# A Mamba mixer: the z products moved into ACT's silu pass, and the D skip moved to its own chunk

## The chip, the cores and the metric

One core of a Trainium2 chip runs the whole kernel in one launch. The metric is the device time in microseconds, lower is better; a number given as "the time" is the median over runs. The engines are PE (TensorE, matrix products), DVE (VectorE), ACT (ScalarE), POOL (GpSimd) and SP (which issues DMAs).

## The reference, cut to what matters

The kernel computes one block of a network on x of shape (8, 1024, 256): a Mamba-2 mixer with an MLP behind it, and then a feed-forward part. The change lies in the mixer:

```
zxbcdt = xn @ in_proj_w                        # z: 512, xBC: 768, dt: 32 columns
xBC = silu(causal_conv1d(xBC, conv_w, conv_b)) # x_ssm 512, B 128, C 128
dt  = softplus(dt + dt_bias)
y   = ssd_scan(xh, dt, B, C, -exp(A_log))      # 32 heads of 16, state 128
y   = y + D_skip * xh
y   = y * silu(z)
y   = y * rsqrt(mean(y*y) + 1e-5) * rms_w
out = y @ out_proj_w + residual
```

Behind it come a layer norm with an MLP (256 to 1024 to 256), and the gated feed-forward part with 1024 hidden units. Products that need full precision are made of three products of rounded halves (high and low parts).

## The kernel before, in words

The mixer (function `mixer`) takes its input in 16 blocks of 512 tokens (two for each of the 8 batch entries) and each block in 4 chunks of 128 tokens. The scan inside a chunk is done as products with a masked decay matrix, for 8 groups of 4 heads; the groups of a chunk are its 8 steps, so a block has 32 steps. The order of the work is written out by hand: each engine runs through the same loop over `S`, with `q, i = divmod(S, 8)` (chunk and step in it) and `n, j = S % 32, S // 32 + 1` (step in the block, and the number of the *next* block, whose preparation is spread over the steps of the present one). Every engine has its own list of what it does in which step; they are joined by semaphores only.

In every step PE makes a decay product (`decay`, L663, into an ebank), ACT takes its exponential into `mh` (`exponent`, L808), DVE masks it (`masked`, L1121), and PE multiplies it with the values five steps later (`intra`, L676, LAG = 5), into the PSUM tile `yin`. `mh` has 7 buffers. Once a chunk, the rest follows: PE `x_by_token` (i = 5), `b_by_token` (i = 6, two products), `to_state` (i = 2, L713) and `from_state` (i = 1, L706); DVE `addends` (i = 1, L1131: yin + dx, where dx is the D skip), `new_state` (i = 0), `square_mean` (i = 6, L1143) and `residual` (i = 7); POOL `gated` (i = 2, L958 and L965: yg, the sum times silu of z); ACT `y_out` (i = 0, L906: the squares); PE `project` (i = 0, L695, and a column of ones over the squares, L698) for the chunk two back; ACT `skip` (L898, four instructions that write dx; i = 3 of the chunk behind its own).

For the next block: two transposes of the normalised input (n = 0, 1), dt (n = 3), six convolution products (n = 5, 7, ..., 15, L650), evacuated by ACT one step later (`conv_in`, L845 and L847), 18 taps of the convolution on DVE (n = 4 to 21, L1076), the products of z (n = 17, 19, 21, 23, also L650), copied out of PSUM by ACT one step later (`keep_z`, L854), the layer norm of the block after (DVE n = 17 to 22, ACT n = 23 and 30), and at n = 26 the silu pass of ACT (`gates`, L858 and L860): silu of z and silu of the convolved xBC, for which ACT changes its function table before and after. `x_by_token` of the next block's first chunk (n = 29) waits for it.

All products that ACT reads go through a ring of three PSUM banks (`ebank`), all that DVE reads through another ring of three (`bank`). `act_bank_order` and `dve_bank_order` list the order in which the banks are given out; PE waits for the bank that was given out three places before.

Of the kernel before, what the change touches and what calls it, by code (L numbers as in the profile page):

```python
# [6 lines left out]
ACT = mybir.ActivationFunctionType  # L7
# [10 lines left out]
NC = HALF // P  # L18
# [3 lines left out]
QI = DI // P  # L22
# [125 lines left out]
WV_AT = 12  # L148
DTW_AT = 19
DTW_READ_AT = 20  # L150
Z_AT = (17, 19, 21, 23)
Z_EVAC_AT = (18, 20, 22, 24)
SILU_AT = 26
TAIL_AT = 22
LN_AT = (17, 20, 21, 22)
# [14 lines left out]
def has_chunk(q):  # L170
    return 0 <= q < CHUNKS


def act_bank_order():

    for S in range(FIRST, LAST):
        q, i = divmod(S, NG)
        n, j = S % SPAN, S // SPAN + 1
        if has_chunk(q):
            yield ("eb", q, i)  # L180
        if i == 1 and has_off(q - 1):
            yield ("ec", q - 1)
        if j < BLOCKS:
            if n in NT_AT:
                yield ("nT", j, NT_AT.index(n))
            if n == DT_AT:
                yield ("dt", j)
            if n in CONV_AT:
                yield ("in", j, QI + CONV_AT.index(n))
            if n == DTW_AT:  # L190
                yield ("dtw", j)
            if n in Z_AT:
                yield ("in", j, Z_AT.index(n))
        if i == 6 and has_chunk(q + 1):
            yield ("bT", q + 1)

# [84 lines left out]
def mixer(nc, ctx, sem, g):  # L281
# [37 lines left out]
    c_yg = Count(sem, "y_gated", 0)  # L319
# [19 lines left out]
    c_xc = Count(sem, "gates_made", 0)  # L339
# [205 lines left out]
    sz = [sb(f"sz{r}", [P, QI, HALF]) for r in range(2)]  # L545
    xc = [sb(f"xc{r}", [P, XM, HALF]) for r in range(2)]

    with ExitStack() as own:
# [9 lines left out]
        def tile(key):  # L558
            return (bank if key in banks.place else ebank)[ring(key).slot(key)]
# [4 lines left out]
        def free(key):  # L564
            return ring(key).free(key)

        def made(eng, key):
            eng.wait_ge(full(key), ring(key).filled(0, key))

        def released(eng, key):  # L570
            eng.wait_ge(free(key), ring(key).used(0, key))
# [74 lines left out]
        def _(pe):  # L646
# [107 lines left out]
            def in_proj(j, m):  # L754
                key = ("in", j, m)
                o = fresh(key)
                for k in range(KD):
                    if m == QI:
                        pe.wait_ge(c_al.sem, c_al.at(0, KD * j + k + 1))
                    mm = product(o[:], [w[:, k, m * P:(m + 1) * P] for w in win], [a[:, k, :] for a in (ah, al)],  # L760
                                 k == 0, k == KD - 1)
                mm.then_inc(full(key), 1)
# [9 lines left out]
            for S in range(FIRST, LAST):  # L772
                q, i = divmod(S, NG)
                n, j = S % SPAN, S // SPAN + 1
                if has_chunk(q):
                    decay(q, i)
                if has_chunk((S - LAG) // NG):
                    intra(*divmod(S - LAG, NG))
                if i == 0 and has_chunk(q - 2):
                    project(q - 2)  # L780
                if i == 1 and has_off(q - 1):
                    state_decay(q - 1)
                    from_state(q - 1)
                if i == 2 and has_state(q - 1):
                    to_state(q - 1)
                if i == 5 and has_chunk(q + 1):
                    x_by_token(q + 1)
                if i == 6 and has_chunk(q + 1):
                    b_by_token(q + 1)
                if j < BLOCKS:  # L790
                    if n in NT_AT:
                        transposes(j, NT_AT.index(n))
                    if n == DT_AT:
                        steps(j)
                    if n in CONV_AT:
                        in_proj(j, QI + CONV_AT.index(n))
                    if n == DTW_AT:
                        weights_by_token(j)
                    if n in Z_AT:
                        in_proj(j, Z_AT.index(n))  # L800

        @block.scalar
        def _(act):
# [42 lines left out]
                                     scale=cw[:, m, TAPS - 1:TAPS])  # L846
                nc.scalar.activation(cin[:, m, TAPS - 1:], tile(key)[:], ACT.Copy).then_inc(free(key), 1)  # L847

            def keep_z(j, m):
                key = ("in", j, m)  # L850
                made(act, key)
                if m == 0 and j >= 2:
                    act.wait_ge(c_yg.sem, c_yg.at(0, NC * (j - 1)))
                nc.scalar.activation(sz[j % 2][:, m, :], tile(key)[:], ACT.Copy).then_inc(free(key), 1)  # L854

            def gates(j):
                released(act, ("in", j, QI - 1))
                nc.scalar.activation(sz[j % 2][:], sz[j % 2][:], ACT.Silu)  # L858
                act.wait_ge(c_conv.sem, c_conv.at(0, XM * (j + 1)))
                nc.scalar.activation(xc[j % 2][:], xc[j % 2][:], ACT.Silu).then_inc(c_xc.sem, 1)  # L860

            def weights(j):
                act.wait_ge(c_cum.sem, c_cum.at(0, j + 1))
# [30 lines left out]
            def skip(q):  # L894
                if q:
                    act.wait_ge(c_yread.sem, c_yread.at(0, q))
                for f in range(QI):
                    ins = nc.scalar.activation(dx[:, f, :], xc[q // NC % 2][:, f, tokens(q)], ACT.Copy,  # L898
                                               scale=dsk[:, f:f + 1])
                ins.then_inc(c_dx.sem, 1)  # L900
# [9 lines left out]
            for S in range(FIRST, LAST):  # L910
                q, i = divmod(S, NG)
                n, j = S % SPAN, S // SPAN + 1
                if has_chunk(q):
                    exponent(q, i)
                if i == 0 and has_chunk(q - 2):
                    y_out(q - 2)
                if i == 2 and has_off(q - 1):
                    state_decay(q - 1)
                if i == 3 and has_chunk(q - 1):
                    skip(q - 1)  # L920
                if i == 7 and has_chunk(q + 1):
                    b_by_token(q + 1)
                if j < BLOCKS:
                    if n in AFFINE_AT:
                        affine(j, AFFINE_AT.index(n))
                    if n == SOFTPLUS_AT:
                        softplus(j)
                    if n in EVAC_AT:
                        conv_in(j, EVAC_AT.index(n))
                    if n == WEXP_AT:  # L930
                        weights(j)
                    if n == DTW_READ_AT:
                        weights_by_token(j)
                    if n in Z_EVAC_AT:
                        keep_z(j, Z_EVAC_AT.index(n))
                    if n == SILU_AT:
                        gates(j)
                if j + 1 < BLOCKS and n in LN_NORM_AT:
                    normalise(j + 1, LN_NORM_AT.index(n))

        @block.gpsimd
        def _(pool):
            def power(turn):
                pool.wait_ge(c_stat.sem, c_stat.at(0, turn))
                pool.tensor_tensor(rstd[:], var[:], neg_half[:, 0:NC], ALU.pow).then_inc(c_rstd.sem, 1)
                pool.wait_ge(c_rstd.sem, c_rstd.at(0, turn))
                pool.tensor_tensor(nmean[:], mneg[:], rstd[:], ALU.mult).then_inc(c_nmean.sem, 1)

            def rms_power(q):
                pool.wait_ge(c_mean.sem, c_mean.at(0, q + 1))  # L950
                pool.tensor_tensor(rms[:], ms[:], neg_half[:, 0:1], ALU.pow).then_inc(c_rms.sem, 1)

            def gated(q):
                added(pool, q)
                if q:
                    made(pool, ("op", q - 1))
                if has_off(q):
                    pool.tensor_tensor(yg[:], yin_s[:], yoff_s[:], ALU.add).then_inc(c_yused.sem, 1)  # L958
                else:
                    pool.sem_inc(s_fill, 1)  # L960
                    pool.tensor_copy(yg[:], yin_s[:]).then_inc(c_yused.sem, 1)
                pool.wait_ge(c_yused.sem, c_yused.at(0, q + 1))
                if q % NC == 0:
                    pool.wait_ge(c_xc.sem, c_xc.at(0, q // NC + 1))
                pool.tensor_tensor(yg[:], yg[:], sz[q // NC % 2][:, :, tokens(q)], ALU.mult).then_inc(c_yg.sem, 1)  # L965

            power(1)
            power(2)
            for S in range(FIRST, LAST):
                q, i = divmod(S, NG)  # L970
                n, j = S % SPAN, S // SPAN + 1
                if j + 1 < BLOCKS and n in LN_POW_AT:
                    power(2 * (j + 1) + LN_POW_AT.index(n) + 1)
                if i == 2 and has_chunk(q - 1):
                    gated(q - 1)
                if i == 6 and has_chunk(q - 1):
                    rms_power(q - 1)
# [826 lines left out]
```

## Time and profile before

| | us |
|---|---|
| median of 3 runs | 3185.32 (3183.98 to 3193.42) |
| the profiled execution, its own time | 3180.88 |
| its span | 3179.2 |
| PE busy | 2799.2 (88%) |
| DVE busy | 1839.9 (58%) |
| ACT busy | 1384.6 (44%) |
| POOL busy | 678.1 (21%) |

The mixer takes the first 1380 us, the MLP and the feed-forward part the rest. Busy times of PE are those of its matmuls as the profile models them: consecutive matmuls overlap, so the distance between two starts is shorter than the duration of one. "idle before, releaser" gives what an engine waited for. PEclk is the granted clock of PE, 1.00 for 2.4 GHz and 0.50 for 1.2 GHz.

### The profile page before, as it was taken

Reading aid. Unit: us, or ns where it says so; the run is one execution under the profiler, and the core shown is the slowest. Engines: PE = TensorE matmul, PEld = TensorE weight load, DVE = VectorE, ACT = ScalarE, POOL = GpSimd, SP = SyncE. Lnnn points to the kernel's source line nnn. Section 1 sums busy time; section 2 is a strip of 40 time slices with the busy share of each in tenths; the row PEclk is TensorE's granted clock in tenths of the full one; section 3 lists DMA queues with packets and bytes.
Section 4 is the critical chain, followed back from the end, with each engine's and each line's share of the span. In section 5 each row is a group of like instructions: output and inputs, shape, how many; then the busy total and the mean of one; then the engine's idle time right before and its main releaser. Section 6 shows DMA issues by size and latency. Waiting matters only on the chain. (4 is left out here: it accounts for less than half of the span.)

```text
span 3179.2 us, 46142 instructions
## 1 busy us (share of the span) xinstructions
PE 2799.2 (88%) x16998; PEld 2086.3 (66%) x16998; DVE 1839.9 (58%) x3504; ACT 1384.6 (44%) x2394; POOL 678.1 (21%) x716
## 2 busy tenths in 40 slices
PE   0488888888888888869999799999999999999999
PEld 0354555455555555458888687887878787878787
DVE  4688888888888888746767433333333333333332
ACT  0566666666666666536555322222222222222221
POOL 5022222222222222210000122222222222222221
PEclk6799989998999899879999899999999999999999
DMA  3010101010101010035211100000000000000000
GB/s 125 29 35 20 35 20 35 20 35 20 35 21 35 21 35 11 28 104 208 70 62 64 48 13 7 11 14 16 14 16 14 16 14 16 14 16 14 16 14 8
DMA packets 104858, 107.06 MB, mean 34 GB/s; under 512 B 35897, under 2 KB 98617, under 8 KB 102977
## 3 DMA queue, kind: packets, MB, share of 16 engines
q1 hardware_dynamic: 99520, 103.81, 10.1%
q8 instruction: 157, 2.57, 0.3%
q10 hardware_dynamic: 5120, 0.19, 0.1%
q14 instruction: 61, 0.49, 0.1%
HBM read 71.41 MB, written 40.94 MB: 35 GB/s over the span
## 5 line engine op out<-in xcount | busy, mean ns | idle before, releaser
L1597 PE MATMUL fbank<-hid,fw 128*128 128x512 f32 x4096 | 962.3, 395 | 0.0
L1597 PEld LDWEIGHTS fbank<-hid,fw 128*128 128x128 f32 x4096 | 766.1, 187 | 187.0
L1747 DVE TENSOR_TENSOR hid<-fhf,hid 128x512 fp32r<-128x512 f32 x384 | 264.9, 690 | 704.3 <-POOL hid L1704 704.3
L1704 POOL TENSOR_SCALAR hid<-fhf 128x512 fp32r<-128x512 f32 x384 | 271.1, 706 | 1040.2 <-ACT fhf L1676 760.8
L808 ACT ACTIVATE mh<-ebank 128x512 f32<-128x512 f32 x512 | 302.0, 598 | 415.0 <-PE ebank L663 413.8
L1121 DVE SCALAR_TENSOR_TENSOR mh<-mh,gm 128x512 f32<-128x512 f32 x512 | 403.2, 794 | 1.8 <-ACT mh L808 1.8
L663 PE MATMUL ebank<-cright,cleft 102*128 102x512 bf16 x512 | 211.1, 413 | 64.1 <-ACT cin L847 28.9
L1676 ACT ACTIVATE fhf<-fbank,sh2c 128x512 f32<-128x512 f32 x128 | 88.0, 688 | 382.4 <-PE fbank L1597 382.4
L676 PE MATMUL yin<-mh,xpad 128*32 128x128 f32 x4096 | 230.5, 300 | 27.1 <-DVE mh L1121 26.6
L650 PE MATMUL ebank<-ah,win 128*128 128x512 f32 x640 | 246.7, 425 | 7.1 <-ACT cin L847 6.6
L1676 ACT ACTIVATE fhf<-fbank,sh1c 128x512 f32<-128x512 f32 x128 | 88.1, 688 | 320.8 <-PE fbank L1597 320.6
L1620 PE MATMUL fbank<-fah,fw 128*128 128x512 f32 x512 | 204.1, 399 | 15.0 <-issue 11.4
L1076 DVE SCALAR_TENSOR_TENSOR xc<-cin,cw,xc 128x512 f32<-128x512 f32 x288 | 214.9, 747 | 0.2
L1620 PE MATMUL fbank<-fal,fw 128*128 128x512 f32 x512 | 202.6, 396 | 0.0
L1667 ACT ACTIVATE sa<-fbank,s1c 128x512 f32<-128x512 f32 x128 | 88.2, 691 | 260.6 <-PE fbank L1620 237.9
L676 PEld LDWEIGHTS yin<-mh,xpad 128*32 128x32 f32 x4096 | 83.6, 111 | 177.4 <-issue 138.4
L1337 PE MATMUL macc<-wm,mhh 128*128 128x256 f32 x1024 | 187.2, 283 | 4.6 <-DVE mhl L1452 3.4
L695 PE MATMUL bank<-wout,yg 128*128 128x256 f32 x512 | 152.6, 450 | 27.5 <-POOL yg L965 27.5
L663 PEld LDWEIGHTS ebank<-cright,cleft 102*128 102x128 bf16 x512 | 54.8, 107 | 176.6 <-issue 72.5
L1337 PE MATMUL mtile<-mah,wm 128*128 128x512 f32 x512 | 166.4, 401 | 1.0 <-DVE mal L1439 1.0
L1337 PEld LDWEIGHTS macc<-wm,mhh 128*128 128x128 f32 x1024 | 157.2, 188 | 8.6 <-DVE mhl L1452 7.1
L650 PEld LDWEIGHTS ebank<-ah,win 128*128 128x128 f32 x640 | 122.6, 192 | 54.0 <-ACT cin L847 13.9
(180 smaller groups left out, 4380.1 us busy)
## 6 DMA issues: line engine op xcount, KB each, us to landing
fx<-x_d SPq DMA_DIRECT2D x17, 512.0 KB, 3.9
xs<-in_x SPq DMA_DIRECT2D x16, 512.0 KB, 4.3
h_d<-in_h SPq DMA_DIRECT2D x16, 512.0 KB, 5.4
o_d<-o SPq DMA_DIRECT2D x16, 512.0 KB, 2.9
mo<-o_d SPq DMA_DIRECT2D x16, 512.0 KB, 3.8
mx<-in_x SPq DMA_DIRECT2D x16, 512.0 KB, 4.8
x_d<-mx SPq DMA_DIRECT2D x16, 512.0 KB, 2.8
fw<-h_d SPq DMA_DIRECT2D x2, 4096.0 KB, 15.2
```

What stands on the lines that cost most here:

```text
L650: mm = pe.matmul(o, left[a], right[c], start=(first and n == 0), stop=(last and n == 2))
L663: pe.matmul(fresh(key)[:], cleft[q // NC % 2][:, q % NC, :], cright[q % 2][:, i // 2 * HQ + i % 2:(i // 2 + 1) * HQ:2, :], start=True, sto ...
L676: mm = pe.matmul(yin[q % 2][row:row + 2 * HD, i // 2, :], xpad[q % 2][:, G4 * (i // 2) + j, i % 2, :, :].rearrange("s w d -> s (w d)"), mh ...
L808: nc.scalar.activation(mh[h_mh.slot((q, i))][:].rearrange("s h t -> s (h t)"), tile(key)[:], ACT.Exp).then_inc(free(key), 1)
L1076: ins = dve.scalar_tensor_tensor(out=xc[j % 2][:, m, :], in0=cin[:, m, t:t + HALF], scalar=cw[:, m, t:t + 1], in1=xc[j % 2][:, m, :], op0= ...
L1121: dve.scalar_tensor_tensor(out=m_[:], in0=m_[:], scalar=1.0, in1=gm[q % 2][:].unsqueeze(1).to_broadcast([P, G4, P]), op0=ALU.min, op1=ALU. ...
L1337: mm = pe.matmul(o, left[i], right[j], start=(first and t == 0), stop=(last and t == 2))
L1597: mm = pe.matmul(bank[banks.slot(key)][:], w[:, k, m * P:(m + 1) * P].bitcast(dt), h[:, k, :].bitcast(dt), start=(k + n == 0), stop=(k == ...
L1620: mm = pe.matmul(bank[banks.slot(key)][:], w[:, k, m * P:(m + 1) * P].bitcast(dt), h[:, k, :].bitcast(dt), start=(k + n == 0), stop=(k == ...
L1676: nc.scalar.activation(hf[j % 3][:], bank[banks.slot(key)][:], ACT.Gelu, scale=s[:, m:m + 1]).then_inc(banks.free(key), 1)
L1704: pool.tensor_scalar(hid[i % 2][0][:, m, :], hf[j % 3][:], 1.0, 0.0, ALU.mult, ALU.add)\
L1747: dve.tensor_tensor(hid[i % 2][1][:, m, :], hf[j % 3][:], hid[i % 2][0][:, m, :].bitcast(F32), ALU.subtract).then_inc(c_lo.sem, 1)
```

## The change

The four products of z are no longer spread over steps 17 to 23 but made one after the other in step 26, behind the other work of PE in that step, and ACT no longer copies them to SBUF: it takes their silu directly from PSUM, behind the silu of xBC, in the same step. The order of the ebanks follows. POOL waits once a block for the last of these instead of for the silu of xBC. The D skip of a chunk is made in step 6 of its own chunk instead of step 3 of the next.

```
-Z_AT = (17, 19, 21, 23)
-Z_EVAC_AT = (18, 20, 22, 24)
@@ act_bank_order
-            if n in Z_AT:
-                yield ("in", j, Z_AT.index(n))
+            if n == SILU_AT:
+                for m in range(QI):
+                    yield ("in", j, m)
@@ tensor
-                    if n in Z_AT:
-                        in_proj(j, Z_AT.index(n))
+                    if n == SILU_AT:
+                        for m in range(QI):
+                            in_proj(j, m)
@@ scalar
-            def keep_z(j, m):
-                key = ("in", j, m)
-                made(act, key)
-                if m == 0 and j >= 2:
-                    act.wait_ge(c_yg.sem, c_yg.at(0, NC * (j - 1)))
-                nc.scalar.activation(sz[j % 2][:, m, :], tile(key)[:], ACT.Copy).then_inc(free(key), 1)
             def gates(j):
-                released(act, ("in", j, QI - 1))
-                nc.scalar.activation(sz[j % 2][:], sz[j % 2][:], ACT.Silu)
                 act.wait_ge(c_conv.sem, c_conv.at(0, XM * (j + 1)))
                 nc.scalar.activation(xc[j % 2][:], xc[j % 2][:], ACT.Silu).then_inc(c_xc.sem, 1)
+                if j >= 2:
+                    act.wait_ge(c_yg.sem, c_yg.at(0, NC * (j - 1)))
+                for m in range(QI):
+                    key = ("in", j, m)
+                    made(act, key)
+                    nc.scalar.activation(sz[j % 2][:, m, :], tile(key)[:], ACT.Silu).then_inc(free(key), 1)
@@ the loop of scalar
-                if i == 3 and has_chunk(q - 1):
-                    skip(q - 1)
+                if i == 6 and has_chunk(q):
+                    skip(q)
-                    if n in Z_EVAC_AT:
-                        keep_z(j, Z_EVAC_AT.index(n))
@@ gpsimd, gated
-                    pool.wait_ge(c_xc.sem, c_xc.at(0, q // NC + 1))
+                    released(pool, ("in", q // NC, QI - 1))
```

## Rows read from the trace of the kernel before

**Rows 1.** Busy time by stretch, the mixer's steady part: us, then each engine.

```profile
128.40:1291.70 1163.30, 980.48 (x7619) 589.57 (x7620) 982.62 (x1938) 764.93 (x1458) 277.47 (x232) 0.91 0.09 28
```

**Rows 2.** Busy time by stretch around T=509.56, same columns.

```profile
497.56:503.56 6.00, 4.53 (x39) 2.21 (x38) 5.81 (x14) 4.41 (x10) 4.61 (x4) 1.00 0.02 5
509.56:515.56 6.00, 2.43 (x29) 0.79 (x28) 4.97 (x15) 5.97 (x4) 2.27 (x3) 0.99 0.00 0
515.56:521.56 6.00, 3.81 (x24) 1.87 (x25) 2.94 (x4) 5.99 (x13) 1.52 (x1) 0.50 0.01 3
```

**Rows 3.** Timeline at T=509.56: start, us, engine, line, instruction, idle before.

```profile
509.56 1.28 ACT L858 ACT_TABLE_LOAD   x1
510.85 1.91 ACT L858 ACTIVATE sz<-sz 128x2048 f32<-128x2048 f32 x1
512.67 2.75 ACT L860 ACTIVATE xc<-xc 128x3072 f32<-128x3072 f32 x1
516.73 0.60 ACT L808 ACTIVATE mh<-ebank 128x512 f32<-128x512 f32 x1
517.22 1.26 ACT L898 ACTIVATE dx<-xc,dsk 128x128 f32<-128x128 f32 x4
518.62 0.69 DVE L1131 TENSOR_TENSOR yin_s<-yin,dx 128x512 f32<-128x512 f32 x1 [3.86 <-ACT dx L898]
```

**Rows 4.** Timeline, projection and mean of squares behind T.

```profile
369.36 0.16 DVE L1143 TENSOR_SCALAR ms<-bank 128x1 f32<-128x1 f32 x1 [2.87 <-PE bank L698]
523.37 3.14 PE L695 MATMUL bank<-wout,yg 128*128 128x256 f32 x8 [0.26 <-POOL yg L965]
527.34 0.16 DVE L1143 TENSOR_SCALAR ms<-bank 128x1 f32<-128x1 f32 x1 [1.95 <-PE bank L698]
```

**Rows 5.** Timeline, one product of in_proj and the decay behind it.

```profile
469.49 0.50 PE L650 MATMUL ebank<-ah,win 128*128 128x512 f32 x1
471.00 0.39 PE L663 MATMUL ebank<-cright,cleft 102*128 102x512 bf16 x1
```

**Rows 6.** Timeline, projection of step 24 and decay of step 26.

```profile
503.55 1.99 PE L695 MATMUL bank<-wout,yg 128*128 128x256 f32 x8 [1.17 <-POOL yg L965]
508.04 0.38 PE L663 MATMUL ebank<-cright,cleft 102*128 102x512 bf16 x1
```

**Rows 7.** Timeline, the evacuation in step 14 and decay 15.

```profile
557.78 0.77 ACT L845 ACTIVATE xc<-ebank,cb,cw 128x512 f32<-128x512 f32 x1
558.45 0.60 ACT L847 ACTIVATE cin<-ebank 128x512 f32<-128x512 f32 x1
559.10 0.39 PE L663 MATMUL ebank<-cright,cleft 102*128 102x512 bf16 x1 [0.96 <-ACT cin L847]
```

**Rows 8.** Busy time by stretch, where the clock fell a second time.

```profile
450.00:454.00 4.00, 2.59 (x28) 1.32 (x26) 1.88 (x3) 3.04 (x6) 0.00 (x0) 1.00 0.00 0
454.00:458.00 4.00, 3.51 (x35) 1.51 (x36) 1.21 (x3) 3.79 (x11) 0.00 (x0) 0.51 0.00 0
```

**Rows 9.** Timeline, last block: projection and decay 26 of the low clock.

```profile
1305.46 3.78 PE L695 MATMUL bank<-wout,yg 128*128 128x256 f32 x8 [0.25 <-POOL yg L965]
1313.92 0.53 PE L663 MATMUL ebank<-cright,cleft 102*128 102x512 bf16 x1
```

**Rows 10.** Timeline, ones, mean of squares and state in steps 14 to 16.

```profile
485.49 0.95 PE L698 MATMUL bank<-ones,ysq 128*128 128x1 f32 x8
486.79 0.15 DVE L1143 TENSOR_SCALAR ms<-bank 128x1 f32<-128x1 f32 x1
491.39 0.69 DVE L1164 TENSOR_TENSOR state<-state,dec 128x512 f32<-128x512 f32 x1 [0.92 <-PE bank L713]
```

**Rows 11.** Timeline, first block: last tap and x_by_token.

```profile
129.05 0.75 DVE L1076 SCALAR_TENSOR_TENSOR xc<-cin,cw,xc 128x512 f32<-128x512 f32 x1
134.28 1.11 PE L723 MATMUL bank<-ident,xc 128*128 128x128 f32 x4 [12.22 <-ACT xc L860]
```

**Rows 12.** Waits of DVE from 128 to 1290 us: total, times, longest.

```profile
DVE yin_s L1131 <- ACT dx L898: 69.8, 25, 3.9
```

## The prediction, written before the result was known

> **What bounds the kernel now.** The page's chain of waits starts at 1812 us, in the last stage, which the change does not touch; the mixer (0 to 1380 us) has to be read by stretches. In its steady part PE is busy 980 and DVE 983 of 1163 us [rows 1]: neither is full, so the question is where each stands idle. The mixer works through 16 blocks of 32 steps, one block about every 78.5 us. I cut a block at T, the moment at which ACT begins the silu pass (table load of L858, step 26). In the window from T-12 to T-6 DVE is busy 5.8 of 6 us and PE 4.5, so DVE sets the pace there; in the 12 us after T PE does 2.4 and 3.8 of 6, DVE 5.0 and 2.9, ACT 6.0, and PE's granted clock is at its lower level, 1.2 GHz (0.50), in the second window [rows 2]. So ACT is the bound from T to T+7.2, and what follows is late because of it.
>
> The chain there: table load, silu of z 1.91 us, silu of xc 2.75 us, table load, and the next exponential starts at T+7.17; then the D skip, and only then DVE's addends of step 25, which had waited 3.86 us for dx, at T+9.06 [rows 3]. From the addends the chain goes on over POOL's yg, PE's projection at 523.37 at the low clock (3.14 us in place of 1.99), the column of ones, to DVE's mean of squares at 527.34, T+17.8 [rows 4]. Over the 14 steady blocks this lasts from 17.8 us (here) to 18.7 (T=350.67, mean of squares at 369.36), 18.1 in the mean; all that comes later follows it.
>
> **The change part by part, for a steady block.**
>
> *1. The z products in the slot of the silu pass (gain).* Before, each z product (6 matmuls) holds PE for 1.51 us from its first matmul to the next decay [rows 5], of which about 1.4 is its own. Now four stand behind to_state of step 26, whose last matmul is given up at about T+0.1, and PE is otherwise waiting there. The ring of three PSUM banks lets three run: done at T+4.4. ACT: load 1.28, silu of xc done at T+4.0 (it was T+5.9), and silu of z from PSUM takes the bank of product 0 until T+4.6. Product 3 needs that bank: T+4.7 to T+6.1, plus some 0.2 until ACT sees it, silu to T+6.9, load to T+8.2: the next exponential is 1.0 us later than before. A silu of 512 columns from PSUM has no row: between 0.48 (a quarter of 1.91) and 0.77 us (the scaled copy into xc, the slowest 512-column row of ACT on these banks [rows 7]); I take 0.6, as the plain copy into cin, its nearest row. Only the first and the last of the four lie on the chain, so the ends differ by 0.6 us a block.
> DVE's addends then wait for PE's intra product of step 23, which PE issues in step 28, two steps (0.7 us each) behind product 3: T+7.6, against T+9.06. The dx wait is gone, because the skip was made in step 22. But from the exponential to ysq ACT has the same list as before (6 exponentials, the skip of the next chunk, now in step 30, the normalisation 2.07): 516.73 to 523.37 (ysq starts with the projection), 6.6 us, hence ysq at T+14.8 and the mean of squares at T+16.6. The projection, ready at T+14.3, is no longer the late one: ysq is. Gain 1.5 us of 18.1. The four copies of z (0.6 each) and the silu of 1.91 us leave ACT; four silus come. None of that ACT time lay on a chain before T, since DVE is full there: worth 0.
>
> *2. The same move thins PE before T (loss).* Of the four products in steps 17, 19, 21 and 23, the last two lay in the 8 us before the projection of step 24. Without them PE cannot go ahead: the intra products of steps 18 and 19 wait for DVE, and the projection waits for POOL's yg, for which PE idled 1.17 us already [rows 6]. In numbers of the view: the window T-12 to T-6 has PE at 4.53 of 6 us [rows 2]; less the 1.4 us of product 3 that is 3.1, and the 6 us before lose two products. The trace shows what such a pace does: over 450 to 454 PE was busy 2.59 of 4 us and the clock was at 0.51 in the next 4 us [rows 8]. So I expect the clock to fall in this stretch in every block, where the run of before held 2.4 GHz. Up to the projection this is free (PE waits anyway). Behind it nothing is: projection, ones, decay 25, ec, from_state, decay 26 and to_state, and with them T, hang on PE. From projection to decay 26 they take 503.55 to 508.04, 4.49 us, at 2.4 GHz and 1305.46 to 1313.92, 8.46 us, at 1.2 GHz [rows 6, 9]: each microsecond at the low level costs 0.47. How long it lasts after the projection differs: at 523.37 it was over within the projection, which lost 3.14 - 1.99 = 1.15 us; at 1305.46 it lasted 8.5 us. I take 5, so T comes 2.3 us later against DVE; ends 1.15 and 2.9 (all 6.1 us up to the z products slow). DVE has its own work up to 514.76 (518.62 - 3.86) and does not feel it before the addends.
>
> A rule speaks here. The row says that the clock fell behind four microseconds in which PE was still busy for more than half [rows 8]. The Trainium skill, "TensorE: Matmul & The Clock Gate", section "Why this matters for your kernels", warns only of long idle gaps between bursts of matmuls; the longest gap I work out is 2.6 us, so by the page the clock would stay. That is the first rival; the trace agrees with it only in so far as the clock did hold with the z products in.
>
> *3. The skip in step 6, 14, 22 and 30 (loss, then a small gain).* Its four ACTs take 1.26 us [rows 3]. In steps 6 and 14 it now stands before the evacuation of a convolution product (conv_in), whose bank PE needs for decay 7 and 15; PE already waits 0.96 us for exactly that [rows 7]. So PE is stopped 1.17 us longer, twice a block: 2.35 us of PE. How much reaches DVE? In the block of T=509.56 the ones end at 486.44 and DVE takes the mean at 486.79: slack 0.35, so DVE loses 2.0 there; but it then idled 0.92 us for PE's to_state in step 16, and half a microsecond more in step 17, and z products 0 and 1, now gone, give PE 2.8 us back by then, so 0.6 stays [rows 10]. In blocks that carry state over, DVE is 2 us behind the ones in step 14, and only new_state of step 8 is late, by 0.7. I take 0.6; ends 0 (all absorbed) and 2.35 (nothing). In step 22 no evacuation stands behind it and in step 30 it is counted in 1. Its new wait, on the addends of step 1, 9, 17, 25, holds back exponential and bT of the next step; by the time ACT is there they are over by 2 us or more, except after T, where they are 2 us over as well. In steps 3, 11, 19 ACT loses 1.26 us of work it had room for; DVE's addends of step 1 no longer wait for dx but for intra 31, 0.2 us earlier.
>
> *4. Ends.* First block: ACT could do silu of z before the last taps (129.05+0.75) were there. Now silu of xc starts at 129.8 and ends at 132.5, but product 3 waits for silu of product 0 (133.1), takes 2.6 us at the low clock, and x_by_token stands behind it on PE: 135.8 instead of 134.28 [rows 11], and ACT's normalisation comes 2 us later; I take +1.8. Last block: the projection started at 1305.46 with the clock low to 1313.9 [rows 9], T+13.8 for T=1291.66; DVE had idled long for dx. Now the projection is not slow, and no normalisation delays ysq: -2.5 with the later T of part 2, -3.7 without it. The waits on yg (ACT) and on the last z bank (POOL, once a block) are long satisfied; no DMA is moved, and SP and POOL keep their order.
>
> **Sum.** -1.5 + 2.3 + 0.6 - 0.2 = +1.2 us a block, 14 blocks +16.8, first +1.8, last -2.5: +16. I shave this to +13, since the last dips (454 to 458 in three of the blocks, 2.6 us each) may also vanish. The profiled execution took 3180.88 us (span 3179.2), 4.4 below the median of 3185.32; the difference of the two kernels is carried over to the median: 3198.
>
> **The rivals.**
> *A, faster: the clock stays at 2.4 GHz before T.* For it: it held at 4.53 of 6 us, and the page's rule. Against: 450 to 454. Then -1.1 a block, -15.4, first +1.8, last -3.7: -17, 3168. It decides at whether the windows from T-12 to T show 1.00.
> *B, clearly slower: PE's stop in steps 7 and 15 is paid whole.* DVE's slack in the trace is 0.35 to 2 us, and in a chain of two full engines idle time is not always recovered. 1.7 more a block: +24 on the forecast, 3222.
> *C, nothing measurable: the clock falls but is back within 3 us of the projection, and the post-T stretch gains what it loses*: +1.15 in place of 2.3: 0.0 a block, about 3185.
>
> **Chances.** A measurement of this kernel tells 0.3% (9.6 us) from no change. Forecast 0.47 (own range 3188 to 3212; a quarter of it lies within 0.3%), A 0.25, B 0.13, C 0.15. Faster 0.25, same 0.27, slower 0.48. The range 3166 to 3222 leaves out the far parts of A and B.
>
> **What would show it.** Right: ACT's next exponential at T+8.2; addends without dx as releaser, at T+7.6 (T of the new run); PE busy through T to T+7 at 1.00; granted clock 0.5 for some microseconds before T-3 and behind the projection of step 24; PE's wait on cin before decay 7 and 15 at 2.1 us; DVE's idle for dx (69.8 us in 25 waits [rows 12]) gone, and its idle before the addends of step 25 at 4 us or more for PE. Wrong: clock 1.00 up to T (A); periods below 78 us; DVE idle of 2 us for the ones of steps 8 and 16 in every block and no recovery (B).

## The result, and the profile after

The changed kernel takes 3244.3 us (median of 4 runs, 3239.6 to 3248.2), the kernel before 3185.7 in the same comparison: ratio 1.018, 95% interval 1.016 to 1.020. It is slower by 58.6 us; 13 were forecast. The profiled execution took 3248.2 us (span 3246.5), 67.3 more than that of before. The last mean of squares of the mixer stands at 1445.1 us, before at 1378.6, so all but 0.8 us of it lies in the mixer. The 14 steady blocks grew by 3.93 us each (78.41 to 82.34), 55.0 together; the start, the first and the last block make up the other 11.5.

The steady part, from the T of the first block to that of the last as in [rows 1] (span, then each engine's busy time, granted clock, DMA share, GB/s):

```profile
core 0: us, PE busy (x) PEld busy (x) DVE busy (x) ACT busy (x) POOL busy (x), PEclk, DMA share, GB/s
128.40:1358.40 1230.00, 1025.02 (x7602) 624.34 (x7602) 985.59 (x1938) 735.88 (x1446) 264.23 (x232) 0.87 0.09 26
```

DVE's busy time is the same to 3 us and ACT's 29 us less; the stretch is 67 us longer. PE is busy 45 us longer with no more instructions, at a clock of 0.87 where it was 0.91. No engine has more to do: one waits more, and PE runs slower.

The stretch behind T of one block, from ACT's and DVE's timelines, for [rows 3] and [rows 4] (start, us, engine, line, instruction, idle before). Here T = 453.99:

```profile
453.99 1.28 ACT L851 ACT_TABLE_LOAD   x1
455.28 2.77 ACT L851 ACTIVATE xc<-xc 128x3072 f32<-128x3072 f32 x1
457.95 1.55 ACT L857 ACTIVATE sz<-ebank 128x512 f32<-128x512 f32 x3
460.29 0.60 ACT L857 ACTIVATE sz<-ebank 128x512 f32<-128x512 f32 x1 [0.78 <-PE ebank L649]
460.90 1.28 ACT L808 ACT_TABLE_LOAD   x1
462.19 2.06 ACT L808 ACTIVATE mh<-ebank 128x512 f32<-128x512 f32 x4
468.36 0.65 ACT L903 ACTIVATE ysq<-yg 128x512 f32<-128x512 f32 x1
461.58 0.69 DVE L1126 TENSOR_TENSOR yin_s<-yin,dx 128x512 f32<-128x512 f32 x1 [5.27 <-PE yin L675]
470.15 0.16 DVE L1138 TENSOR_SCALAR ms<-bank 128x1 f32<-128x1 f32 x1 [1.81 <-PE bank L697]
```

This went as forecast: the next exponential at T+8.2, ACT idle for the fourth product only, the addends at T+7.6 without dx as releaser, ysq at T+14.4 as the late one, the mean of squares at T+16.2.

The stretch ahead of T, from PE's timeline, for [rows 6], and by windows, for [rows 2]:

```profile
444.02 3.78 PE L694 MATMUL bank<-wout,yg 128*128 128x256 f32 x8 [2.33 <-POOL yg L960]
449.16 0.59 PE L662 MATMUL ebank<-cright,cleft 102*128 102x512 bf16 x1
452.47 0.38 PE L662 MATMUL ebank<-cright,cleft 102*128 102x512 bf16 x1
```

```profile
434.80:438.80 4.00, 2.02 (x21) 1.04 (x17) 3.84 (x12) 2.99 (x9) 0.00 (x0) 1.00 0.01 2
438.80:452.40 13.60, 10.22 (x54) 7.31 (x55) 13.38 (x31) 3.78 (x7) 5.69 (x6) 0.50 0.01 3
454.00:460.00 6.00, 5.87 (x25) 4.24 (x23) 1.98 (x3) 5.50 (x5) 0.00 (x0) 1.00 0.00 0
```

PE was busy 2.02 of the 4 us before, and then its clock stands at its lower level, 1.2 GHz, from 438.8 to 452.4, and the chain from projection to decay 26 takes 8.45 us, the whole of what [rows 9] show at that level, not the middle between that and 4.49. The low clock behind T is gone in exchange. And in step 7, from the timelines of ACT and PE, for [rows 7]:

```profile
419.42 1.26 ACT L895 ACTIVATE dx<-xc,dsk 128x128 f32<-128x128 f32 x4
421.25 0.58 ACT L847 ACTIVATE cin<-ebank 128x512 f32<-128x512 f32 x1
421.89 0.61 PE L662 MATMUL ebank<-cright,cleft 102*128 102x512 bf16 x1 [2.12 <-ACT cin L847]
```

PE waits 2.12 us for the evacuation, as forecast. But the decay behind the wait takes 0.61 us in place of 0.39: the clock fell there too, from 421.7 to 425.1. Nothing in the prediction foresaw that.

Where the 3.93 us lie, by DVE's order of work (means over the 14 steady blocks, worked out from the starts of mask, addends and mean of squares in each trace; the last columns are the projection of step 24 to T, then T to the addends of step 25 and to the mean of squares of step 30; "low" is time at 1.2 GHz up to T-12, from there to T, and behind T). Each row is one profiled execution. For the experiments I give the same table at once:

```
kernel                     steps 0-8  8-16  16-24  to add.  to ms | block | proj-T  T-add.  T-ms | low
before                        21.85  18.20  20.97    6.68   9.11 | 78.41 |   6.01    9.06  18.17 | 1.5  0.0 12.1
the change                    22.72  19.65  20.91    8.97   8.50 | 82.34 |   9.78    7.72  16.22 | 9.0 10.3  0.2
z only                        23.05  18.16  20.51   11.05  10.02 | 84.39 |   9.47   10.11  20.13 | 7.4 10.0  8.5
skip only, ahead              22.12  19.74  23.04    2.62  11.08 | 80.21 |   6.01    4.96  16.04 | 5.1  0.0 10.2
z, skip behind                21.69  18.16  20.47    7.68   8.50 | 78.11 |   8.58    7.60  16.10 | 4.4  8.7  0.0
z, ahead in step 6 only       23.05  18.68  20.52    9.16   8.50 | 81.50 |   9.97    7.72  16.22 | 7.6 10.7  0.2
z, ahead in step 14 only      21.70  18.80  21.02    6.80   8.50 | 78.43 |   7.73    7.60  16.11 | 5.1  7.1  0.0
change + 4 fillers            22.50  19.44  22.57    5.85   8.51 | 80.46 |   6.73    7.61  16.11 | 4.9  1.5  0.0
z, skip behind, 4 fillers     21.78  18.17  21.00    5.37   8.50 | 76.42 |   6.25    7.60  16.11 | 1.9  0.5  0.1
z, skip behind, 2 fillers     21.72  18.18  20.46    5.71   8.50 | 76.17 |   6.54    7.60  16.10 | 1.9  4.3  0.1
skip behind, z old, xc first  21.45  18.17  20.71    2.58  10.57 | 75.08 |   6.01    4.97  15.53 | 0.0  0.0  8.5
skip behind, z old            22.03  18.24  21.32    2.58  11.01 | 76.77 |   6.01    4.96  15.97 | 3.4  0.0  8.8
```

Each row adds up to the block with 1.60 us more, from the mean of squares to the next block.

### The profile page after: what moved, and what is told of

It is laid out like the page before. It is cut to its first block and busy times, and to the rows that moved or that the text cites. A ratio compares the mean times of both kernels' runs of the same rounds, so it can differ in the third digit from the quotient of the medians.

```text
span 3246.5 us, 46126 instructions
## 1 busy us (share of the span) xinstructions
PE 2850.2 (88%) x16998; PEld 2129.0 (66%) x16998; DVE 1842.7 (57%) x3504; ACT 1352.4 (42%) x2378; POOL 663.2 (20%) x716
## 3 DMA queue, kind: packets, MB, share of 16 engines
q8 instruction: 157, 2.57, 0.3%
## 5 line engine op out<-in xcount | busy, mean ns | idle before, releaser
L649 PE MATMUL ebank<-ah,win 128*128 128x512 f32 x640 | 259.9, 456 | 17.8 <-ACT sz L857 9.5
L694 PE MATMUL bank<-wout,yg 128*128 128x256 f32 x512 | 164.3, 476 | 50.3 <-POOL yg L960 50.3
L649 PEld LDWEIGHTS ebank<-ah,win 128*128 128x128 f32 x640 | 131.8, 206 | 74.9 <-ACT sz L857 16.9
L694 PEld LDWEIGHTS bank<-wout,yg 128*128 128x128 f32 x512 | 115.1, 237 | 87.4 <-POOL yg L960 62.1
```

The source lines that it names most:

```text
L649: mm = pe.matmul(o, left[a], right[c], start=(first and n == 0), stop=(last and n == 2))
L694: pe.matmul(o[:, 0:D], yg[:, f, :], wout[:, f, :], start=(f == 0), stop=(f == QI - 1))
```

## The experiments

Theory 1 is the prediction's mechanism, theory 2 the rival named with each run. "The change" is the kernel after. "The stop" is PE's wait of 2.1 us for the copy into cin ahead of decay 7 or 15, named after ACT's step 6 or 14, in which the skip stands ahead of that copy ("the evacuation"). Times are medians. The kernel before was run again beside experiments 1 to 4 (3189.9 us), 5 to 8 (3190.3) and 9 and 10 (3185.1), so a difference between runs of two of these groups can be off by some 5 us.

**1. The z products alone.** The skip goes back to step 3 of the next chunk:

```
-                if i == 6 and has_chunk(q):
-                    skip(q)
+                if i == 3 and has_chunk(q - 1):
+                    skip(q - 1)
```

> The z products and the silu of z moved as in the change, the D skip left in step 3 of the next chunk. Theory 1 (PE thinned before the silu pass: the clock falls to 0.50 before the projection of step 24 and T comes 3.8 us late in each of 14 blocks; the skip's place costs another 2.3 us in steps 0 to 16): steps 0 to 16 as in the run before (40.0 us in the mean of the steady blocks, not 42.4), the clock low from T-12 to T as in the run of the change, but the addends wait for dx again (T+10 instead of T+7.7): 3235 to 3250 us. Theory 2 (the stop of PE in steps 7 and 15 by the skip is the cause of nearly all, the clock included): 3185 to 3200 us and the clock at 1.00 before T.

Measured 3274.8 us, ratio 1.027 (1.025 to 1.029). Theory 1 had the sign and missed the size (3235 to 3250). With the skip behind the longer silu pass, from the timelines of ACT and DVE (T = 453.81):

```profile
462.02 0.60 ACT L808 ACTIVATE mh<-ebank 128x512 f32<-128x512 f32 x1
462.51 1.26 ACT L895 ACTIVATE dx<-xc,dsk 128x128 f32<-128x128 f32 x4
463.91 0.69 DVE L1126 TENSOR_TENSOR yin_s<-yin,dx 128x512 f32<-128x512 f32 x1 [6.97 <-ACT dx L895]
```

the addends come at T+10.1 and the mean of squares at T+20.1, 1.0 and 2.0 us later than before. The z move by itself gains nothing behind T. Steps 0 to 8 lose 1.2 us too, which theory 1 had unchanged: PE's clock falls 12.2 to 13.3 us behind T, and in 12 of the 14 blocks it is still low when the next block begins.

**2. The skip alone**, in step 6 of its own chunk, with z as before (the change's hunks on z undone).

> Only the D skip moved (step 6 of its own chunk), z as in the kernel before. Theory 1: PE waits 2.1 us for cin in steps 7 and 15, steps 0 to 16 are 1 to 2.3 us longer per block, the clock stays at 1.00 before T, the addends of step 25 no longer wait for dx (T+5.3): 3190 to 3215 us. Theory 2: most of the 58 us, 3230 us or more.

Measured 3210.7 us, ratio 1.007 (1.005 to 1.010), as theory 1 had it. The table shows both sides of it: behind T the block gains 2.1 us (T to mean of squares 16.04), more than the whole change does, and steps 0 to 24 lose 3.9.

This run also separates the stop from the clock. The stop in step 6 is in all 14 steady blocks. In 7 of them the clock falls behind it for 3.4 us; there steps 0 to 8 take 22.8 us and DVE waits 1.25 us for the ones. In the other 7 the clock holds; they take 21.45 us and DVE does not wait, as in experiment 8, which has no stop (21.45). One block of each kind, first without the fall, from the timelines of PE and DVE:

```profile
312.13 0.39 PE L663 MATMUL ebank<-cright,cleft 102*128 102x512 bf16 x1 [2.12 <-ACT cin L847]
318.01 0.15 DVE L1143 TENSOR_SCALAR ms<-bank 128x1 f32<-128x1 f32 x1
```

```profile
390.73 0.39 PE L663 MATMUL ebank<-cright,cleft 102*128 102x512 bf16 x1 [2.12 <-ACT cin L847]
397.95 0.16 DVE L1143 TENSOR_SCALAR ms<-bank 128x1 f32<-128x1 f32 x1 [1.27 <-PE bank L698]
```

and by windows up to and behind the end of the stop, in the same order:

```profile
309.10:312.10 3.00, 0.91 (x12) 0.47 (x11) 2.93 (x6) 2.91 (x7) 1.27 (x1) 1.00 0.00 0
312.10:317.00 4.90, 4.87 (x35) 3.37 (x35) 4.80 (x13) 3.03 (x6) 0.00 (x0) 1.00 0.04 8
387.70:390.70 3.00, 0.91 (x12) 0.47 (x11) 2.93 (x7) 2.91 (x7) 1.26 (x1) 1.00 0.00 0
390.70:395.60 4.90, 4.87 (x27) 2.74 (x28) 4.80 (x13) 2.37 (x5) 0.00 (x0) 0.68 0.04 8
```

PE was busy 0.91 of 3 us up to the end of both stops. What decides whether the clock falls behind one stays open. Behind the stop in step 14 it falls in all 14 blocks.

**3. The change, with the skip behind the evacuation.** One call moves down in ACT's list, so that in steps 6 and 14 the copy into cin comes first:

```
-                if i == 6 and has_chunk(q):
-                    skip(q)
                 if i == 7 and has_chunk(q + 1):
...
                     if n == SILU_AT:
                         gates(j)
+                if i == 6 and has_chunk(q):
+                    skip(q)
```

> The whole change, but in steps 6 and 14 ACT makes the D skip behind the evacuation of the convolution product instead of ahead of it. Theory 1: PE's wait for cin is 0.96 us again and steps 0 to 16 give back about 2 us per block, the clock before T is as low as in the change: 3210 to 3220 us. Theory 2: 3185 to 3195 us.

Measured 3181.6 us (10 runs), ratio 0.997 (0.996 to 0.998). Neither theory had it: 62.7 us of the changed kernel hang on the place of four instructions of 1.3 us together. PE's wait for cin over the steady part, first in the change and then in this kernel (engine, tile, line, releaser: total, times, longest):

```profile
PE ebank L662 <- ACT cin L847: 63.5, 30, 2.1
```

```profile
PE ebank L662 <- ACT cin L847: 28.8, 30, 1.0
```

The wait for cin shrinks by 34.7 us and the kernel by 62.7. So the stop costs nearly twice itself; runs 9 and 10 take that up.

**4. Is it the thinned PE that makes T late?** The change, with a filler in steps 18, 20, 22 and 24: six matmuls of the weights into the bank that the next decay overwrites. The output does not change; PE has back what the z products were to its clock.

```
+            def filler(q, i, j):
+                o = tile(("eb", q, i))
+                pe.wait_ge(free(("eb", q, i)), ring(("eb", q, i)).used_before(0, ("eb", q, i)))
+                for k in range(KD):
+                    product(o[:], [w[:, k, 0:P] for w in win], [a[:, k, :] for a in (ah, al)],
+                            k == 0, k == KD - 1)
...
+                if has_chunk(q) and j < BLOCKS and n in (18, 20, 22, 24):
+                    filler(q, i, j)
```

> The whole change, and in steps 18, 20, 22 and 24 PE makes a product of six matmuls of the size of a z product into the bank of that step's decay, ahead of the decay product that overwrites it: its result is used nowhere. It restores PE's load ahead of the silu pass, with nothing for ACT or the ring. Theory 1: the clock stays at 1.00 from T-12 to T, projection of step 24 to T takes 6 us again instead of 9.8, though PE does 5.8 us more work per block: 3190 to 3205 us. A theory in which the burst in step 26 or the skip is what costs (rivals 2 and 3): no gain, 3240 to 3260 us.

Measured 3212.1 us, ratio 1.007 (1.005 to 1.009): useless work makes the kernel 32 us faster. It is 7 us above theory 1's range; the fillers themselves cost 1.7 us in steps 16 to 24. PE's timeline:

```profile
440.78 1.99 PE L694 MATMUL bank<-wout,yg 128*128 128x256 f32 x8 [1.63 <-POOL yg L969]
443.42 0.38 PE L662 MATMUL ebank<-cright,cleft 102*128 102x512 bf16 x1
445.26 0.38 PE L662 MATMUL ebank<-cright,cleft 102*128 102x512 bf16 x1
```

Projection to decay 26 takes 4.48 us, as in [rows 6], and low time in the 12 us before T falls from 10.3 to 1.5 us. This shows the mechanism of part 2 of the prediction: PE's load ahead of T sets how late T comes.

**5. The kernel before, with the skip behind the evacuation**, and z as it was.

> The kernel before with only the D skip moved to step 6 of its own chunk, but behind the evacuation (z in its old steps). Theory 1 (the skip's place ahead of the evacuation stops PE; its removal from step 27 frees DVE's addends): steps 0 to 24 as before (61 us), from there to the mean of squares 13.7 us as in the run with the skip alone, instead of 15.8: 3155 to 3165 us. Rival (what gains in the third run is the z products in the silu slot): 3185 to 3190 us.

Measured 3139.3 us (5 runs, 3137.0 to 3160.2), ratio 0.984 (0.982 to 0.986): the half of the change that is worth having, and 16 us below theory 1's range (3155 to 3165). Its profiled execution is the one of 3160.2 us, 21 above the median: in 7 of its 14 steady blocks the clock is low for 6.8 us in steps 1 and 2, and steps 0 to 24 take 61.6 us in the mean where experiment 8 has 60.3. The kernel before has that dip in 3 blocks. So the row to hold against the others is that of experiment 8, the same kernel but for the order within the pass. Against experiment 3, the z move costs 42 us.

**6. Experiment 3 with the four fillers.**

> The change with the skip behind the evacuation and the filler products in steps 18, 20, 22 and 24 (results unused). Theory 1: projection of step 24 to T takes 6 us instead of 8.6, the clock is at 1.00 before T, period 76 us: 3150 to 3160 us. If the low clock before T is not on the path, 3180 us.

Measured 3157.0 us, ratio 0.990 (0.988 to 0.993). Held.

**7. The same with fillers in steps 22 and 24 only.**

> As the run before it in this list, with the filler products in steps 22 and 24 alone. Theory 1: half the extra work is enough to keep the clock up to the projection, since the thinned stretch lies between step 21 and the projection of step 24: 3150 to 3165 us, and 16 to 24 as without fillers. If the clock needs the load of steps 17 to 20 too, it is low for part of the stretch: 3165 to 3180 us.

Measured 3145.1 us, ratio 0.986 (0.984 to 0.988), below the range. Two fillers cost steps 16 to 24 nothing (20.46) and shorten the low stretch enough:

```profile
410.00:416.00 6.00, 2.75 (x27) 1.31 (x25) 5.81 (x17) 2.52 (x7) 0.97 (x1) 1.00 0.02 4
416.00:422.00 6.00, 5.22 (x24) 3.26 (x21) 6.00 (x9) 3.19 (x6) 3.64 (x4) 0.58 0.00 0
422.00:428.00 6.00, 6.00 (x45) 4.22 (x45) 5.81 (x18) 1.88 (x4) 0.86 (x2) 0.85 0.00 0
```

T is 427.80 there. The clock falls a few microseconds before the projection of 419.85 and is up again by decay 25. So of the 42 us that the z move costs with the skip behind, 36 come back with PE's load before T; in the profiled executions it is 30 us, 27 of them in the steady blocks, and projection to T is 2.04 us shorter in each of these (29 us).

**8. Experiment 5 with silu of xc ahead of silu of z** (the two lines of `gates` change places, and POOL waits for the second by a semaphore of its own). It asks whether the order within the pass was worth anything.

> The kernel before with the skip behind the evacuation, and in the silu pass xc ahead of z (z in its old steps, one silu of 2048 columns in SBUF; POOL waits for the silu of z). Theory 1: x_by_token comes 1.9 us earlier, but the exponential of step 27 as late as in the run without this, and DVE waits for that: equal within 3 us to the first run of this list. If x_by_token was on the path, 10 to 25 us less than it.

Measured 3139.2 us, ratio 0.986 (0.982 to 0.990), the same as experiment 5. ACT's and DVE's timelines (T = 423.49):

```profile
424.78 2.76 ACT L858 ACTIVATE xc<-xc 128x3072 f32<-128x3072 f32 x1
427.45 1.89 ACT L860 ACTIVATE sz<-sz 128x2048 f32<-128x2048 f32 x1
429.37 1.28 ACT L808 ACT_TABLE_LOAD   x1
428.67 0.68 DVE L1131 TENSOR_TENSOR yin_s<-yin,dx 128x512 f32<-128x512 f32 x1
438.73 0.16 DVE L1143 TENSOR_SCALAR ms<-bank 128x1 f32<-128x1 f32 x1 [3.31 <-PE bank L698]
```

Here is the cleanest look at the skip: with dx made in step 22 and no z products on PE, DVE's addends start without any wait at T+5.2 (5.0 in the mean, 4.1 earlier than before).

**9 and 10. Which stop is dear?** Experiment 3 with the skip ahead of the evacuation in one step alone:

```
+                if n == 6 and has_chunk(q):      # n == 14 in experiment 10
+                    skip(q)
                 if i == 7 and has_chunk(q + 1):
...
-                if i == 6 and has_chunk(q):
+                if i == 6 and n != 6 and has_chunk(q):
                     skip(q)
```

> The change with the skip behind the evacuation in step 14 (as in the third experiment) but ahead of it in step 6 only. Between the third experiment (3181.6) and the change (3244.3) lie 62.7 us. Theory 1 (each of the two stops of 1.17 us reaches DVE whole, 14 x 1.17 = 16 us each, and the rest, some 30 us, is clock time and the last block, which both stops bring about together): this kernel at 3198 to 3215. Theory 2 (the stop in step 6 is the harmless one, since PE stands ahead of DVE there and only new_state of step 8 hangs on it; step 14, with the column of ones of the projection, carries nearly all): 3180 to 3190.

> The change with the skip ahead of the evacuation in step 14 only, behind it in step 6. Theory 1 (both stops pass through alike): 3198 to 3215, and the two single prices add up to at most the 62.7 us of the pair. Theory 2 (step 14 carries nearly all): 3230 to 3245.

Measured 3231.2 us for step 6, ratio 1.014 (1.012 to 1.016), and 3188.5 us for step 14 (10 runs), 1.001 (1.000 to 1.002). Both theories fall, and the second the wrong way round: the stop that I held for harmless costs 50 us, the other 7. (Each against the kernel before of its own comparison, it is 54 and 12.) The two traces of the same block, first experiment 3, then experiment 9; PE's timeline, with ACT's skip:

```profile
385.59 1.28 ACT L895 ACTIVATE dx<-xc,dsk 128x128 f32<-128x128 f32 x4
385.76 0.39 PE L662 MATMUL ebank<-cright,cleft 102*128 102x512 bf16 x1 [0.96 <-ACT cin L847]
387.94 0.39 PE L662 MATMUL ebank<-cright,cleft 102*128 102x512 bf16 x1
```

```profile
394.84 1.26 ACT L895 ACTIVATE dx<-xc,dsk 128x128 f32<-128x128 f32 x4
397.31 0.61 PE L662 MATMUL ebank<-cright,cleft 102*128 102x512 bf16 x1 [2.12 <-ACT cin L847]
400.89 0.39 PE L662 MATMUL ebank<-cright,cleft 102*128 102x512 bf16 x1
```

and the windows before and behind the end of the stop, in the same order:

```profile
382.10:385.50 3.40, 2.66 (x18) 1.25 (x16) 3.37 (x4) 1.64 (x4) 2.89 (x2) 1.00 0.00 0
385.50:388.90 3.40, 3.14 (x25) 1.83 (x26) 3.33 (x9) 2.55 (x9) 0.00 (x0) 1.00 0.04 7
```

```profile
393.70:397.10 3.40, 1.50 (x14) 0.61 (x12) 3.33 (x6) 2.75 (x7) 1.77 (x2) 1.00 0.00 0
397.10:400.50 3.40, 3.19 (x14) 2.00 (x15) 3.33 (x10) 0.92 (x3) 0.00 (x0) 0.51 0.06 12
```

With the stop PE is busy 1.50 of 3.4 us where it was 2.66, and the next 3.4 us run at 0.51. From decay 7 to decay 8, with one convolution product between, it is 3.58 us in place of 2.18. The stop is 1.16 us longer and what follows it 1.40 slower: 2.56 us. What that does to DVE, in the two timelines:

```profile
390.45 0.95 PE L697 MATMUL bank<-ones,ysq 128*128 128x1 f32 x8
392.80 0.15 DVE L1138 TENSOR_SCALAR ms<-bank 128x1 f32<-128x1 f32 x1
```

```profile
403.40 0.95 PE L697 MATMUL bank<-ones,ysq 128*128 128x1 f32 x8
404.39 0.16 DVE L1140 TENSOR_SCALAR ms<-bank 128x1 f32<-128x1 f32 x1 [1.12 <-PE bank L697]
```

In experiment 3 the ones end at 391.40 and DVE takes them 1.40 us later. That slack covers a stop of 1.16 us and not one of 2.56: DVE waits 1.12. A low stretch of 3.4 us in steps 3 to 6 by DVE's count stands in 12 of the 14 blocks of experiment 9 and in none of experiment 3. In one of the two blocks without it steps 0 to 8 take 21.45 us, as in experiment 3 (21.44), with the stop as long as elsewhere; in the other DVE waits 0.26 us for the ones. With the two kinds of block of experiment 2 this shows that the stop in step 6 by itself all but fits into DVE's slack, and that the low clock behind it is what DVE pays for. Experiment 9 then loses 0.52 us in steps 8 to 16, and 1.48 at T, where the low stretch is mostly 13.7 us and was 10.2 in half of the blocks. Experiment 10 loses 1.19 us in steps 8 to 24 and gets 0.88 back before the addends, where its low stretch is shorter (projection to T 7.73 after 8.58). Its clock falls too, for 3.4 us behind the stop in all 14 blocks. The 1.19 is a mean of 0.6 us in every second block and 1.7 in the others, so that it is near the stop's 1.16 says nothing. Why the low stretch before T is longer in the one and shorter in the other stays open; I made no run on it.

## Why the prediction was wrong

**The bound** was read rightly: the stretch behind T goes by ACT's pass, then by ysq, and DVE sets the pace ahead of it.

**Part 1, -1.5 us.** Measured 18.17 to 16.22, -1.95; all its marks (T+8.2, T+7.6, ysq the late one) came. But the gain was booked to the wrong edit: it stands under the z products, and it is the skip's. Without the z move it is 2.1 to 2.6 us (experiments 2 and 8), with the z move alone it is a loss of 2.0 (experiment 1). In the combination the z move takes back 2.6 us at the addends (T+7.60 after T+4.97) and 0.6 at the mean of squares. The prediction compared with before only, where dx hid what the fourth product costs. The silu from PSUM took 0.59 us, where 0.6 was taken.

**Part 2, +2.3 us.** The mechanism is shown by experiments 4, 6 and 7. Measured 3.77 from the projection to T, above the end of 2.9: I took 5 us of low clock behind the projection, and it stayed low for all of the way to decay 26 (8.45 us). With the skip behind, it is 2.57, within 1.15 to 2.9; the rest comes with the stop in step 6 (3.96 with that stop alone, 1.72 with the other alone), by a longer low stretch whose cause is open. Rival A is ruled out. The row of before that spoke for the fall (2.59 busy of 4 us) was the one to go by, and the changed kernel has 2.02 of 4. PE's longest wait there was 2.56 us, on DVE's mask, where 2.6 was worked out. The Trainium skill, "TensorE: Matmul & The Clock Gate", section "Why this matters for your kernels", warns of long idle gaps only; by that the clock would have stayed, and the granted clock of 0.50 from 438.8 to 452.4 says otherwise, so the measurement decides.

**Part 3, +0.6 - 0.2: the step that failed.** "So 0.6 stays": measured, steps 0 to 24 lose 2.26 us against before, and against the same kernel with the skip behind the evacuation the place of the skip costs 4.23 us a block (82.34 - 78.11), 2.52 of it in steps 0 to 16, 0.44 in 16 to 24 and 1.29 at T. Even the end that I gave for "paid whole", 2.35, was too low. Two things were wrong in it. For step 14 I let the z products' time absorb the stop, and it did so in part: against the same kernel without the stop, steps 8 to 24 lose 3.6 us with the z products in place (experiment 2) and 1.2 without them (experiment 10). That is still more than the 0.6 that I left for both stops. For step 6 the slack was there (1.40 us against 1.16, and DVE loses nothing in 8 of the 9 blocks of experiments 2 and 9 where the clock holds) and the clock took it away: I had asked in part 2 what a thinned PE does to its clock, and not in part 3, where PE stands still for 2.1 us. That is also where rival B fell short: it had the place and the direction, 3222 us, and a price without the clock. Its own mark, DVE idle for the ones of both steps in every block, was not the one that decided: most of the price sits in step 6 and at T. The -0.2 beside the 0.6 was not measured apart.

**Part 4.** -0.7 was taken for the two ends, +11.5 measured. The first block's mask starts 2.4 us later (+1.8 was taken; the fourth product waited 9.5 us for silu of product 0, as described). The first block is 5.3 us longer (75.8 to 81.1), which was not priced. Behind the last T the fast projection came: up to the last block's first mask it is 3.9 us less (20.7 to 16.8). But the last block itself grew by 3.75 us (66.2 to 70.0), which was not priced either. With the skip behind it takes 63.9 us in experiment 3 and 68.0 and 68.3 in experiments 7 and 8, so the skip's place alone does not explain it; that stays open.

**The shave** from 16 to 13 went the wrong way: the dips of 6.8 us in step 1 of three blocks became dips of 3.4 us at the start of seven, and those behind the stops came on top.

The sum by measured terms: -1.95 (T to mean of squares) + 3.77 (projection to T) + 2.32 (steps 0 to 16) - 0.06 (16 to 24) = 4.08, against 3.93 for the block; the 0.15 between them is the way from step 24's mask to its projection.

Of the whole, with round numbers from the runs: the skip in its own chunk, behind the evacuation, -51; the z move on top of it, +42 (36 of it come back with fillers before T); the skip ahead of the evacuation in step 6, +50, and in step 14, the rest, +13 (7 alone). These are differences of medians taken one after the other, so they add up by construction, to 54; the 4.6 missing from 58.6 are the difference between the two medians of the kernel before (3185.7 and 3190.3). The version to keep is experiment 5, 1.6% faster than before and 105 us faster than the change.

## What to carry to other kernels

- A wait put on PE can have two prices: its length, and the clock behind it. If another stretch of the trace lost its clock with PE about as busy as around the new wait, price the work behind the wait once at each clock level, and only then subtract slack. Here the stop in step 6 fitted into the slack, and the clock behind it did not.
- Compare blocks of one run with each other before making a new run: experiment 2 held blocks with the fall and blocks without it behind the same stop.
- Moving work off PE into its idle time is no gain in itself: the products that "cost" DVE nothing before T were what held the clock for the chain behind them. With the skip behind the evacuation, two fillers of six matmuls were worth 36 us.
- Cost two edits that meet in one wait in both orders. Here one alone explained the gain, and the other took part of it back. And within a step, work that nobody waits for goes behind what another engine waits for.

## What was new about the hardware

- PE's clock fell for 3.4 us behind a stop of 2.1 us in 12 of 14 blocks of experiment 9, in all 14 of experiment 10 and in 7 of 14 behind the stop in step 6 of experiment 2, and behind none of the stops of 0.96 us in experiment 3. With PE busy 0.91 of the 3 us up to the end of the stop, it fell in one block of experiment 2 and held in another.
- In experiment 7 PE was busy 2.75 of 6 us at 2.4 GHz, then 5.22 of 6 with the clock low for most of them (0.58), then all 6 with the clock mostly back (0.85).
- An ACT function table took 1.28 us to load at every one of the places shown, whatever stood around it.
- Silu of 512 columns from PSUM took ACT 0.59 us, the same as a plain copy from PSUM into cin (0.58 to 0.60).
